# Last stage: every second tile shifted by VectorE, its exponentials one operation; three perceptrons' down products in three passes over parts

## The reference

```
L0:  h = ln(x);            x += attn(h -> ctx) @ cproj;        x += gelu(ln(x) @ fc_w)  @ proj_w
L1:  h = x / rms(x) ...;   x  = attn(x -> [ctx, x]) @ out_w;   x += gelu(norm(x) @ mlp_w1) @ mlp_w2
L2:  two attentions of 16 heads of 128;                        x += gelu(ln(x) @ w_fc1) @ w_fc2     # "M2"
L3:  self attention (L3s), cross attention (L3c), 16 heads of 16:
       scores = q @ k.T / 4;  scores = scores * mask - 10000 * (1 - mask)
       probs  = softmax(scores);  x += (probs @ v) @ w
     x += gelu(ln(x) @ w1) @ w2                                                                     # "L3c mlp"
```

## Time and profile before

| | |
|---|---|
| time, median of 3 runs | 1022.51 us (1022.27 to 1022.55) |
| the profiled execution, its own time | 1022.81 us |
| its span in the profile | 1021.6 us |
| busy share of the span | PE 98%, DVE 78%, ACT 57%, POOL 65% |
| mean granted TensorE clock | 1.00 (of 2.4 GHz) |

### The profile page before, as it was taken

The page is one execution under the profiler, slowest core; times in us unless marked ns, Lnnn a source line. Parts: engine busy times, 40 slices in busy tenths (PEclk is TensorE's granted clock), DMA queues, the critical chain, the costliest instruction groups (busy, mean ns, idle before and its releaser), DMA issues.

```text
span 1021.6 us, 21422 instructions
## 1 busy us (share of the span) xinstructions
PE 998.7 (98%) x8252; PEld 899.9 (88%) x8252; DVE 796.9 (78%) x1289; ACT 582.1 (57%) x1289; POOL 664.0 (65%) x691
## 2 busy tenths in 40 slices
PE   7899999999999999999999999999998999999998
PEld 6788878888989999999998999999998989877887
DVE  7998888999257677988868878888985388999771
ACT  5989888887535324233233332223235479999982
POOL 6796576447667888556368988666637367677541
PEclk9999999999999999999999999999999999999999
DMA  8200001000121221211121111100140000000000
GB/s 338 116 2 2 1 2 43 2 1 2 47 78 32 61 61 46 63 43 43 42 77 31 42 42 32 42 27 27 32 166 1 2 1 1 3 2 2 12 12 21
DMA packets 34221, 40.74 MB, mean 40 GB/s; under 512 B 2159, under 2 KB 31305, under 8 KB 32713
## 3 DMA queue, kind: packets, MB, share of 16 engines
q1 hardware_dynamic: 34121, 39.38, 11.6%
HBM read 38.32 MB, written 1.05 MB: 39 GB/s over the span
## 4 chain that ended last, share of the span: by engine, by line
PE 84%; ACT 6%; DVE 5%; POOL 3%; issue 1%; DMA 1%; SPq 0%; POOLq 0%; DVEq 0%; ACTq 0%
PE psum L829 11%; PE psum L965 10%; PE psum L1031 8%; PE psum L983 8%; PE psum L813 8%; PE psum L856 6%; PE psum L1018 5%; PE psum L997 5%; PE psum L950 4%; PE psum L845 3%; PE psum L741 3%; PE psum L871 3%; PE psum L1007 3%; PE psum L898 2%; PE psum L797 2%; ACT C tile L1624 2%
## 5 line engine op out<-in xcount | busy, mean ns | idle before, releaser
L1879 POOL TENSOR_TENSOR A tile<-A tile,outer rec 128x1024 f32<-128x1024 f32 x48 | 90.3, 1895 | 74.3 <-DVE outer rec L1229 74.1
L2028 POOL TENSOR_TENSOR B tile<-B tile,B rec 128x1024 f32<-128x1024 f32 x32 | 61.0, 1912 | 102.1 <-DVE B rec L1400 102.1
L1720 ACT COPY B PT<-psum 128x512 f32<-128x512 f32 x64 | 33.0, 600 | 138.0 <-PE psum L1007 138.0
L1624 ACT ACTIVATE A tile<-A tile,outer min 128x128 f32<-128x128 f32 (+1 forms) x256 | 91.7, 446 | 0.8 <-DVE outer min L1220 0.7
L1624 ACT ACTIVATE C tile<-C tile,outer min 128x128 f32<-128x128 f32 x256 | 77.8, 401 | 0.5 <-DVE outer min L1220 0.4
L983 PE MATMUL psum<-B v hi,cT hi 128*128 128x256 f32 x256 | 72.1, 282 | 0.3 <-ACT B kT L1539 0.3
L983 PE MATMUL psum<-B v hi,cT lo 128*128 128x256 f32 x256 | 71.7, 280 | 0.0
L983 PE MATMUL psum<-B v lo,cT hi 128*128 128x256 f32 x256 | 71.7, 280 | 0.0
L1590 ACT COPY A PT<-psum 128x512 f32<-128x512 f32 x96 | 51.4, 589 | 21.4 <-PE psum L856 14.7
L1213 DVE TENSOR_TENSOR A tile<-m,psum 128x1024 f32<-128x1024 f32 x48 | 56.4, 1215 | 8.8 <-PE psum L845 7.0
L1018 PEld LDWEIGHTS psum<-B PT,B v 128*128 128x128 f32 x512 | 59.4, 192 | 1.1
(11 more groups left out here) (364 smaller groups left out, 3526.6 us busy)
## 6 DMA issues: line engine op xcount, KB each, us to landing
raw<-in_wq SPq DMA_DIRECT2D x32, 128.0 KB, 2.7
raw<-in_wk SPq DMA_DIRECT2D x32, 128.0 KB, 3.0
raw<-in_wv SPq DMA_DIRECT2D x16, 256.0 KB, 2.8
raw<-in_wo SPq DMA_DIRECT2D x16, 256.0 KB, 2.7
weights<-in_weights_c SPq DMA_DIRECT2D x4, 1024.0 KB, 5.8
weights<-in_weights_a SPq DMA_DIRECT2D x1, 3072.0 KB, 21.1
weights<-in_weights_a SPq DMA_DIRECT2D x1, 2048.0 KB, 11.0
wide<-in_bias_v SPq DMA_DIRECT2D x2, 1024.0 KB, 8.8
```

The costliest lines, as they stand in the source:

```text
L1624: i = act.activation(of_head, of_head, ACT.Exp, bias=part.min[:, u % 4, h:h + 1], scale=-1.0)
L1879: pool.tensor_tensor(tile(u, ly.nk), tile(u, ly.nk), part.rec[:, u % 4, 0:ly.per].unsqueeze(2).to_broadcast([P, ly.per, ly.nk]), ALU.mult) ...
L2028: pool.tensor_tensor(tv, tv, m.brec[:, h, :].unsqueeze(2).to_broadcast([P, B, S]), ALU.mult).then_inc(s["normalised"].sem, s["normalised"] ...
```

## The change

Two things are done, and the lists of the first and the last part are written anew around them.

**The tiles.** In the last part, for tile `r` = 0 of each unit, DVE subtracts the minimum of each head from the tile in one more instruction, with the minima spread over the tile. ACT then makes the exponentials of the whole tile in one instruction without a bias in place of eight. For tile `r` = 1 all stays.

**The down products** of L1, M2 and L3c (L0's stay). POOL cuts the down weights in two parts (`cut_down`, 4 pairs of a cast and a subtraction for each perceptron) and, after ACT's gelu, every pair of chunks of `aT` as well (`split`, 16 pairs for each perceptron). PE multiplies the parts in three passes, each one instruction: 24 instructions where 16 were. A `down` waits for POOL's split of each pair of chunks, not for ACT alone. M2 has one buffer `aT` in place of two, since its parts take the room of the other. The four `cut L3c` move from the end of the middle part into the last part; four `cut_down M2` stand in their place.

```diff
+def shifted_whole(st, r):
+    return st == "C" and r == 0
...
             dve.tensor_reduce(part.min[:, u % 4, 0:ly.per], tile(u, ly.nk), AX.X, ALU.min).then_inc(s["min_made"].sem, s["min_made"].mark((st, u)))
+            if shifted_whole(st, r):
+                dve.wait_ge(s["min_made"].sem, s["min_made"].at((st, u)))
+                dve.tensor_tensor(tile(u, ly.nk), tile(u, ly.nk), part.min[:, u % 4, 0:ly.per].unsqueeze(2).to_broadcast([P, ly.per, ly.nk]),
+                                  ALU.subtract).then_inc(s["shifted"].sem, s["shifted"].mark((st, u)))
...
+            if shifted_whole(st, r):
+                act.wait_ge(s["shifted"].sem, s["shifted"].at((st, u)))
+                act.activation(part.tiles[u % 4][:, :], part.tiles[u % 4][:, :], ACT.Exp, scale=-1.0).then_inc(s["exp_made"].sem, s["exp_made"].mark((st, u)))
+                return
...
-            pe.wait_ge(s["up_drained"].sem, s["up_drained"].at((name, "up", k, FC - 2)))
-            for c in range(FC):
-                i = pe.matmul(bank(z)[:, 0:D], part.aT(k)[:, c, b * P:(b + 1) * P], w2[:, c, :], start=c == 0, stop=c == FC - 1)
+                hi, lo = part.aT_hi(name, k), part.aT_lo(name, k)
+                for c in range(FC):
+                    if c % 2 == 0:
+                        pe.wait_ge(s["w2_lo_made"].sem, s["w2_lo_made"].at((name, c // 2)))
+                        pe.wait_ge(s["aT_lo_made"].sem, s["aT_lo_made"].at((name, k, c)))
+                    a = hi[c // 2][:, c % 2, b * P:(b + 1) * P], lo[:, c, b * P:(b + 1) * P]
+                    w = m.w2_hi[name][c // 2][:, c % 2, :], m.w_lo[UP[name][2]][:, c, :]
+                    for ap, wp in PASSES:
+                        i = pe.matmul(bank(z)[:, 0:D], a[ap], w[wp], start=(c, ap, wp) == (0, 0, 0), stop=c == FC - 1 and ap == 1)
...
+        def split(name, k, o):
...
+            pool.wait_ge(s["up_drained"].sem, s["up_drained"].at((name, "up", k, o)))
+            pool.tensor_copy(part.aT_hi(name, k)[o // 2][:, :, :], part.aT(name, k)[:, of, :]).then_inc(
+                s["aT_hi_made"].sem, s["aT_hi_made"].mark(event))
+            pool.wait_ge(s["aT_hi_made"].sem, s["aT_hi_made"].at(event))
+            pool.tensor_tensor(part.aT_lo(name, k)[:, of, :], part.aT(name, k)[:, of, :], part.aT_hi(name, k)[o // 2][:, :, :], ALU.subtract).then_inc(
+                s["aT_lo_made"].sem, s["aT_lo_made"].mark(event))
```

More of the change, by code:

```diff
@@ L249, in split @@
         self.hi = [sb(f"{t}h hi{k}", [P, C, T], F32R, where) for k in range(NS)]
+        self.aT_parts = [sb(f"{t}aT part{k}", [P, FC, T], F32R, where) for k in range(len(self.aTs))]
     def h(self, k):
@@ L537 @@
[L537 to L540 removed]
+    ctx 0 5, turn_in L0 in 0 3, ctx 1 0, q L0 0 1, k L0 0 0 3, k L0 1 0 7, ctx 2 4, scores 0, k L0 2 0 4, v L0 2 0 7, turn_in L0 in 1 5, scores 1,
@@ L574 @@
[L574 to L577 removed]
+    stats L0 in 0, xn L0 in 0, ctx 0 5, wcut L0 k, ctx 1 0, stats L0 in 1, q L0 0 1, stats L0 in 2, stats L0 in 3, ctx 2 4, scores 0, minima 0,
@@ new lines @@
+    down L1 0 1 2, project 17 0, project 19 4, stats L1 mlp 2, stats L1 out 0, scores 22, minima 22, scores 23, minima 23, even 22 0, even 22 1,
+    turn_in L1 mlp 2 7, even 23 0, down L1 1 0 1, down L1 1 1 0, even 23 1, weigh 21, stats L1 out 1, weigh 23, project 21 0, project 23 2,
+    stats L1 mlp 3, down L1 2 0 7, down L1 2 1 0, stats L1 out 2, turn_in L1 mlp 3 4, parts 0, parts 1, down L1 3 0 1, down L1 3 1 2, stats L1 out 3,
+    parts 2, parts 3, values_of 0, values_of 1, values_of 2, values_of 3, queries_of 1
@@ L1900, in do @@
                 cut_up(*a)
+            elif what == "cut_down":
+                cut_down(*a)
+            elif what == "up" and a[0] != "L0":
+                split(*a[:3])
             elif what == "wcut" and tuple(a) != ("L0", "k"):
```

292 lines of the change are left out of this document (163 added, 129 removed).

## The result

The changed kernel takes 1055.34 us (median of 4 runs, 1054.48 to 1055.76) beside 1022.53 us of the kernel before (1022.27 to 1022.65): a ratio of 1.0317, 95% interval 1.0305 to 1.0329. It is slower, as forecast, but by 32.8 us in place of 10.5, and outside the range that ended at 1044. The profiled execution has a span of 1053.9 us.

What follows compares the result with a forecast made beforehand. DVE, with ACT beside it, was taken to bound the middle stretch, PE most of the rest: 1021.6 - 4.2 - 1.9 + 10.5 + 5.8 = 1031.8 us of span, plus 1.2: 1033.0 us; range 1015 to 1044.

Steps and rivals of the forecast that it cites:

- What bounds the kernel: From `scores 2` to `scores 15` (middle stretch, 133.0 us) DVE works 120.5 us, over 90%, with ACT beside it.
- PE's time: All 24 `down` in three passes: 0.62 us less each, 14.9 us in all, 9.9 of it in the last part.
- The wait between VectorE and GpSimd: Middle stretch: each two-input subtraction waits for POOL's instruction in hand, 0.85 us, 13 times: 11.0 us.
- The sum of the middle stretch: `scores 2` to `scores 15`: DVE's 138.8 us plus 11.0 of waits, less 6.2, is 143.6 us for 133.0: +10.5.
- The 6.2 us that "don't count": End of middle stretch: DVE's steps between its masks of units 14 and 15, taken as not delaying `scores 15`.
- The first part: PE busy 295 of 305 us, so L1's 5.0 us count in full, less 0.8 for last splits: -4.2 us.
- Cover enough: First part: POOL gets 20 pairs, 38 us on 200 of 305, and still has room.
- Ahead of `scores 2`: PE has 2.3 us less work; waits are 5.0 us where about 4.6 stood before: -1.9 us.
- After `scores 15`: PE all but full; work moved behind the middle stretch adds 5.7 us, waits 0.1: +5.8 us.
- (a): Rival: subtractions find POOL between instructions, the 11.0 us go: 1022.0 us; chance 0.21 together with a case between.
- (b): Rival: DVE's steps fit under PE everywhere, so all 14.9 us of PE's gain stay: 1007.9 us; chance 0.09.
- (c): Rival: POOL's splits come late among masks in the last part, end 7 us behind the sum: 1040 us; chance 0.17.

Runs made afterwards that it cites:

- one-input run: Changed kernel with the subtraction replaced by an equally long second reduction with one input (output not the reference's): 1033.36 us.
- float32-down kernel: Changed kernel with its lists and subtraction, but all down products in float32, without cuts or splits: 1053.89 us.
- the other execution: The changed kernel run once more, unchanged, for a second trace: 1053.96 us.
- on the old lists: Kernel before plus only the tile 0 shift, with one-input reduction in place of the subtraction: 1034.72 us, against 1042.18 with the subtraction.

## Why the prediction was right or wrong

**What bounds the kernel.** Right: the middle stretch is VectorE's. It is busy 145.85 of 150.98 us, and PE idle for 27 us there. PE's own work fell by less than the 13.3 us forecast: from 128.4 to 119.0 at the full clock, in the one-input run.

**PE's time.** Right in size. Three `down` in a row took 10.37 us for 48 instructions, and now:

```profile
1041.66 8.44 PE psum L862 x72
```

That is 2.81 us for one, forecast 2.83 and 2.84. The Trainium skill (FP8 and Floating Point Precision, TensorE Precision Notes) counts four passes for true FP32; three in place of four would have made it 2.60, by an estimate from these four and the 3.46. The trace shows less gain than that.

**The wait between VectorE and GpSimd.** Right in kind and nearly in size: 0.85 us for a subtraction against (28.5 - 13 x 1.22) / 13 = 0.97. The upper bound of one mask was wrong: the instruction at 879.83 us took 3.4 us longer than alone, beside the rest of one mask, the whole of the next and a cast. GpSimd's part was right in kind: 9.5 us more in the stretch, about 0.7 for each subtraction, where I had up to 1.1.

**The sum of the middle stretch.** Wrong by 7.5 us, and the end of VectorE's masks of unit 14 splits the error. I let VectorE work and wait without a gap up to there, 138.8 + 11.0 - 6.2 = 143.6 us behind `scores 2`, and PE start `scores 15` at that moment. Measured: VectorE is busy 144.2 us up to there, idle 4.5 us, and PE starts 2.3 us later: 151.0.

So work and waits together were off by 0.6 us, in part by luck: 130.6 us of work in the one-input run where I had 132.6, and 13.6 of waits where I had 11.0. The 6.2 us that "don't count" mostly didn't: of the 7.0 us that VectorE works between its masks of units 14 and 15, 1.7 lie ahead of `scores 15`. The steps that failed are **two terms put at nothing**. One is VectorE's idle time, 4.5 us in pieces of 1.0 us at most, 1.5 in all for PE's output products. The other is "PE may start `scores 15` as soon as DVE has done its masks of unit 14". VectorE has done them at 994.05 us, and PE still has steps of its own list ahead, L3c's `down` among them. VectorE, and then PE:

```profile
991.74 2.31 DVE L1244 TENSOR_TENSOR C tile<-psum,wide 128x1024 f32<-128x1024 f32 x2
```

```profile
990.36 1.15 PE L878 MATMUL psum<-C kT,C qT 32*128 32x256 f32 x16
...
995.01 0.48 PE L862 MATMUL psum<-weights lo 128*128 128x256 f32 x2 [0.36 <-POOL C aT part L1885]
...
996.33 1.15 PE L878 MATMUL psum<-C kT,C qT 32*128 32x256 f32 x16
```

GpSimd's splits are not what holds it: PE waits 0.36 us for them in this `down`, and in the float32-down kernel, which has none, `scores 15` stands the same 6.0 us behind `scores 14`, and 2.3 behind VectorE's masks:

```profile
985.90 1.15 PE L882 MATMUL psum<-C kT,C qT 32*128 32x256 f32 x16
...
987.91 3.62 PE L856 MATMUL psum<-weights,C aT 128*128 128x256 f32 x16
...
991.90 1.15 PE L882 MATMUL psum<-C kT,C qT 32*128 32x256 f32 x16
```

A stretch between two steps of PE ends where PE's own list lets it, and I had taken the end from one of the engines that feed it. What is also new: PE is at a lower granted clock in places where it waits much, which the prediction called "no term here". Between 885 and 915 us:

```profile
885.00:895.00 10.00, 6.82 (x68) 5.45 (x68) 9.86 (x21) 7.54 (x21) 8.74 (x12) 0.94 0.00 0
895.00:905.00 10.00, 8.65 (x96) 6.67 (x96) 9.08 (x22) 5.29 (x11) 6.72 (x10) 0.89 0.01 2
905.00:915.00 10.00, 7.04 (x61) 5.83 (x62) 8.97 (x9) 6.50 (x16) 6.58 (x6) 0.83 0.01 2
```

A value under 1 is a mean of the two levels, 2.4 and 1.2 GHz, over the window. It makes PE's work 4.7 us longer in the stretch (123.75 against 119.01 with one input). How much of that lengthens the stretch stays open: it is contained in the 16.1 us of the second input, with the 13.6 us of VectorE.

**The first part.** The largest miss, 9.5 us, and the step that failed is a term that wasn't there. I counted the passes (5.0, less 0.8) and took the new lists as free because PE was busy 295 of 305 us. In float32 they cost 3.7 us even in an execution without a long encounter (330.0 us, the float32-down kernel): PE is busy 1.2 us and idle 2.5 us more. The passes gave back 2.8 of it (327.2), not 4.2. Their 4.9 us arrive at the last down product, but the way out then goes by GpSimd and VectorE. "Cover enough" for GpSimd was thus wrong too: in the changed kernel it is busy without a gap from 273.1 to 289.7 us, and the residual that VectorE waits for stands behind the splits, though to move it ahead of them changed nothing. The profiled execution has another 4.4 us: `B hT lo` beside the value bias (2.3), everything ahead of it 0.6 later, and PE behind it at a granted clock of 0.83 between 300 and 310 us (5.96 us for 4.33, 1.6). I had read the same encounter at 285.68 us in the trace of before and used it for the last part only.

**Ahead of `scores 2`.** Forecast -1.9, measured +1.2. PE's busy time fell by 1.3 us (55.70 to 54.38), not 2.3, and its idle time rose from 2.9 to 5.4 us, 2.8 of it waits for splits. The waits that I found in the new list, 5.0 us, were thus nearly right. The step that failed is what I took off them, "about 4.6" for the kernel before: the earlier trace rows has 63.68 us with PE busy for 60.75, so 2.9. With one input the head is 58.7, so 1.1 us go with the second input. The 61.4 of the other execution has 1.7 us more of PE's busy time, at a lower clock.

**After `scores 15`.** +7.9 for +5.8. The work moved behind was priced well: PE's busy time rose by 6.0 us. The rest is that PE isn't full at once: its idle time is 5.6 us where it was 3.7, and the chain runs through VectorE and GpSimd to 1010.4 us.

**Rivals.** (a) and (b) fell: VectorE and GpSimd meet often, and PE's gain arrives in part only. (c), GpSimd late, had the right sign for its splits: PE waits 4.3 us for them in all, and more than 3 was one of my signs of being wrong. But without splits, and with the subtraction, the kernel is only 1.4 us faster, so its 7 us on top of my sum aren't what was missing, and its 1040 us was too low as well.

**The range.** Its top, 1044, was (c) with some more: my sum plus one mishap. The four stretches missed in the same direction. In each a new order was taken at the busy time of the engine that I held for the bound, with little or nothing for what that engine waits for.

## What to carry to other kernels

A new order of the lists is a change of its own: price it separately from the edit that it was made for, stretch by stretch, from what stands ahead of each critical step in every engine's queue. When an edit puts an instruction with two SBUF inputs on VectorE beside a busy GpSimd, count the wait on both engines, look for places where GpSimd has several long instructions in a row, and ask whether one input can come from PSUM or be left out. A run with a stand-in of equal length and one input tells what the pairing costs: here 22 us of 33, and on the old lists, with GpSimd less busy, 7.5 of 20. And price an order of lists from more than one execution: here the same first part took 330.0 and 333.1 us.

## What the hardware showed that I hadn't expected

- The two engines don't take strict turns. A VectorE instruction took 4.66 us for 1.22, beside the rest of one GpSimd instruction, all of the next and most of a third. The pair `B hT lo`, 128x512 each, took 4.4 to 6.7 us in executions of the same program, beside one GpSimd instruction of 4.6 us and those behind it.
- It reaches the other engines: with the second input gone PE's matmuls in the middle stretch ran at a granted clock of 1.00 in place of 0.97, and PE was idle for 15.8 us in place of 27.2.
- The masks of GpSimd at 128x1024, which take 2.4 us for themselves, were hardly lengthened (2411 to 2406 and 2492 ns); its two-input instructions of 128x512 were, from 1.28 us with one input on VectorE to 1.52, the longest 2.28. The losses on GpSimd's side fell on the short instructions behind the masks.
